# Row maxima of an attention kernel: split as columns, turned by the DVE, and started eight units earlier

## What is computed

```python
Q, K, V = (proj(Wq), proj(Wk), proj(Wv))          # x is (8, 512, 1024); 16 heads of 32
att = jnp.einsum('bhqd,bhkd->bhqk', Q, K) * (1.0 / math.sqrt(Dh)) + b[0]
att = att * m + (1.0 - m) * NEG_INF               # m: mask over the keys
att = jax.nn.softmax(att, axis=-1)
y = jnp.einsum('bhqk,bhkd->bhqd', att, V)         # then y back to (B, C, T)
q, in_scale = per_token_quant_int8(y)             # FFN: absmax per row, int8
out = (q @ weight.T) * in_scale * w_scale + bias  # cast to float16
return x + out
```

## Time and profile before

| | |
|---|---|
| median of 3 runs | 2440.25 us (2439.67 to 2441.79) |
| the profiled execution | 2440.84 us, of it 2439.0 us span from the first to the last instruction |
| TensorE busy | 2387.2 us, 98% of the span, at a mean granted clock of 0.993 |
| POOL, DVE, ScalarE busy | 1672.1, 1560.4 and 1346.3 us (69%, 64% and 55%) |
| chain of work that ended last | TensorE 67% of the span, DMA 4%, POOL and DVE 2% each |

### The profile page before, as it was taken

One profiled execution on the slowest core, in us unless ns is written; L12 is line 12 of the kernel. 1 busy time (PEld: TensorE's weight loads), 2 busy tenths in 40 slices (PEclk: granted clock), 3 DMA queues, 4 the chain that ended last, 5 costly groups with the idle time before them and its releaser, 6 DMA issues.

```text
span 2439.0 us, 37390 instructions
## 1 busy us (share of the span) xinstructions
PE 2387.2 (98%) x12376; PEld 1341.0 (55%) x12376; DVE 1560.4 (64%) x1683; ACT 1346.3 (55%) x2536; POOL 1672.1 (69%) x677
## 2 busy tenths in 40 slices
PE   8999999997999999999999999999999999999996
PEld 7888888884444444444444444444444444444442
DVE  3311111145777777777777777777777877777771
ACT  3222222214666666666666666666666666666664
POOL 3322223414778888888877888888788888887777
PEclk9999999998999999999999999999999999999999
DMA  6655555365677776777677777666776667776751
GB/s 243 252 200 199 214 193 195 147 211 126 147 160 160 157 157 147 157 159 159 151 159 159 156 160 156 157 151 150 160 160 155 155 150 160 160 155 154 157 111 44
DMA packets 143498, 396.55 MB, mean 163 GB/s; under 512 B 14584, under 2 KB 50424, under 8 KB 127296
## 3 DMA queue, kind: packets, MB, share of 16 engines
q0 software_dynamic: 18144, 132.13, 27.4%
q10 hardware_dynamic: 49312, 130.80, 22.8%
q1 hardware_dynamic: 75968, 132.74, 14.9%
HBM read 161.51 MB, written 100.93 MB: 108 GB/s over the span
## 4 chain that ended last, share of the span: by engine, by line
PE 67%; DMA 4%; issue 2%; POOL 2%; DVE 2%; ACT 0%; SPq 0%; ACTq 0%; POOLq 0%; DVEq 0%
PE score L689 21%; PE pv L716 18%; PE ring L127 18%; PE ring L749 4%; DMA q_stack<-max_lo 4%; PE ring L726 2%; PE ring L729 2%; DVE neg_max L136 1%; PE ring L740 1%; POOL acc L988 1%; PE ring L734 0%; DMA probs<-probs 0%; POOL acc L1000 0%; ACT probs L798 0%; SPq L609 0%
## 5 line engine op out<-in xcount | busy, mean ns | idle before, releaser
L798 ACT ACTIVATE probs<-score 128x512 f32<-128x512 f32 x2048 | 1074.7, 604 | 576.4 <-PE score L689 559.5
L136 DVE TENSOR_REDUCE neg_max<-ring 128x1 f32<-128x1024 f32 x1024 | 1208.4, 1220 | 230.8 <-PE ring L127 219.1
L689 PE MATMUL score<-q_stack,k_stack 100*128 100x512 f32 x2048 | 875.8, 429 | 23.9 <-DMA q_stack<-max_lo 16.6
L988 POOL TENSOR_TENSOR acc<-acc,probs 128x2048 f32<-128x2048 f32 x189 | 867.1, 4588 | 26.6 <-DMA probs<-probs 11.9
L127 PE MATMUL ring<-k_stack,q_stack 98*128 98x512 f32 x2048 | 810.6, 396 | 0.3 <-DVE neg_max L136 0.2
L689 PEld LDWEIGHTS score<-q_stack,k_stack 100*128 100x128 f32 x2048 | 387.3, 189 | 504.0 <-ACT probs L798 358.2
L716 PE MATMUL pv<-probs,v_in 128*32 128x512 f32 x4096 | 546.1, 605 | 0.0
L127 PEld LDWEIGHTS ring<-k_stack,q_stack 98*128 98x128 f32 x2048 | 390.8, 191 | 66.6 <-DVE neg_max L136 0.8
L988 POOL TENSOR_TENSOR acc<-probs 128x2048 f32<-128x2048 f32 x63 | 288.8, 4584 | 100.8 <-DMA probs<-probs 100.8
L479 POOL TENSOR_TENSOR q_stack<-x_raw,k_stack 128x1024 fp32r<-128x1024 f32 x28 | 67.7, 2450 | 294.7 <-ACT k_stack L364 294.7
L972 POOL DMA_DIRECT2D probs<-probs x126 | 108.2, 859 | 175.4 <-PE pv L716 168.2
(11 more groups left out here) (95 smaller groups left out, 2026.6 us busy)
## 6 DMA issues: line engine op xcount, KB each, us to landing
probs<-probs POOLq DMA_DIRECT2D x126, 1024.0 KB, 8.0
k_stack<-qk_part ACTq DMA_DIRECT2D x93, 512.0 KB
q_stack<-qk_part ACTq DMA_DIRECT2D x183, 256.0 KB, 5.4
qk_part<-part_hi SPq DMA_DIRECT2D x64, 512.0 KB, 2.6
qk_part<-part_lo SPq DMA_DIRECT2D x64, 512.0 KB, 3.5
v_steps<-v_out SPq DMA_DIRECT2D x64, 256.0 KB, 2.2
res<-x ACTq DMA_DIRECT2D x32, 512.0 KB, 5.7
out<-res SPq DMA_DIRECT2D x64, 256.0 KB, 2.1
```

The costliest lines, as they stand in the source:

```text
L136: nc.vector.tensor_reduce(neg_max[:, pair // CHUNK, pair % CHUNK:pair % CHUNK + 1], ring[:, :], AX_X, ALU.max, negate=True).then_inc(neg_m ...
L689: pe.matmul(score[score_bank(t)][:, :], k_stack[par][0:ROWS, h, kt * P:(kt + 1) * P], q_stack[par][0:ROWS, half, h, :], start=True, stop=T ...
L798: nc.scalar.activation(probs[:, kt, h, :], score[score_bank(t)][:, :], ACT.Exp).then_inc(exp_done, 1)
L988: nc.gpsimd.tensor_tensor(acc[:, half, :, :], first, probs[:, tile, :, :], ALU.add).then_inc(acc_done, 1)
```

## The change

OWN becomes 12, so each pair is made eight units earlier: 52 units of the step before hold pairs of a step, where 44 did. Chunk 1 is complete after unit 11 of its own step, chunk 0 after unit 43 of the step before. TensorE no longer turns the maxima. ScalarE and the DVE split the columns of `neg_max` where they stand (128 partitions by 16 columns), the DVE turns the two parts together, in blocks of 32 by 32, and SP writes them with four DMAs for each chunk, one for each 32 partitions. Before attention begins, 26 pairs are made where 22 were.

```diff
-OWN = 20
+OWN = 12
 EARLY = (UNITS - OWN) // 2
+MAXIMA_1, MAXIMA_0 = OWN - 1, OWN + UNITS // 2 - 1
...
+                    for pair in range(TT * 3 * CT // 4, EARLY):
+                        pe.wait_ge(neg_max_done, pair - 1)
+                        for half in range(2):
+                            row_max(pe, ring[pair % 2], q_stack, k_stack, 0, pair, half, rowmax_done)
...
-                for part, rows in ((0, max_hi), (1, max_lo)):
-                    dst = q_stack[par][ROW_MAX + part:ROW_MAX + part + 1, chunk, :, :]
-                    sp.dma_start(dst.bitcast(F32), rows[:, chunk, :].bitcast(F32)).then_inc(max_rows[chunk], 16)
+                rows = q_stack[par][ROW_MAX:ROW_MAX + 2, chunk, :, :].rearrange("r h (a g j) -> r h a g j", g=P // DH, j=DH)
+                for g in range(P // DH):
+                    sp.dma_start(rows[:, :, :, g, :].bitcast(F32), max_turned[g * DH:(g + 1) * DH, chunk, :]).then_inc(max_rows[chunk], 16)
...
-            def turn_max(s, chunk, buf):
-                pe.wait_ge(neg_max_done, PAIRS * s + CHUNK * (chunk + 1))
-                pe.transpose(buf[0:CHUNK, N:N + P], neg_max[:, chunk, :], ident[:, :]).then_inc(maxT_done, 1)
-
...
-            def high_max(s, chunk, buf):
-                act.wait_ge(maxT_done, 2 * s + chunk + 1)
-                wait(act, max_rows[chunk], MAX_ROWS * s)
-                nc.scalar.activation(max_hi[:, chunk, :], buf[0:CHUNK, N:N + P], ACT.Copy).then_inc(max_hi_done, 1)
+            def high_max(s, chunk):
+                act.wait_ge(neg_max_done, PAIRS * s + CHUNK * (chunk + 1))
+                wait(act, max_turn_done, 2 * (s - 1) + chunk + 1)
+                nc.scalar.activation(max_parts[:, chunk, 0, :], neg_max[:, chunk, :], ACT.Copy).then_inc(max_hi_done, 1)
...
-                    if t == SUMS_1 and main:
-                        high_max(s, 1, ring_of(par, ("extra", SUMS_1)))
+                    if t == MAXIMA_1 + 3 and main:
+                        high_max(s, 1)
...
+            def turn_max(s, chunk):
+
+                dve.wait_ge(max_lo_done, 2 * s + chunk + 1)
+                wait(dve, max_rows[chunk], MAX_ROWS * s)
+                nc.vector.transpose(max_turned[:, chunk, :],
+                                    max_parts[:, chunk, :, :].rearrange("p a b -> p (a b)").bitcast(F32)).then_inc(max_turn_done, 1)
...
-                    if t == SUMS_1 and main:
-                        low_max(s, 1, ring_of(par, ("extra", SUMS_1)))
+                    if t == MAXIMA_1 + 2 and main:
+                        low_max(s, 1)
+                        turn_max(s, 1)
+                    if t == MAXIMA_0 + 2 and ahead:
+                        low_max(s + 1, 0)
+                        turn_max(s + 1, 0)
```

More of the change, by code:

```diff
@@ L659, in wait_ring @@
                 elif t in (SUMS_1, SUMS_0):
-                    wait(pe, sums_out, 2 * s + (t == SUMS_0))
-                    if not isinstance(s, int) or s + (t == SUMS_0) < STEPS:
-                        pe.wait_ge(max_lo_done, 2 * s + (2 if t == SUMS_1 else 3))
+                    pe.wait_ge(sums_out, 2 * s + (t == SUMS_0))
                 elif t == TURN_Q:
@@ L671, in take_ring @@
                     pe.wait_ge(neg_max_done, EARLY)
-                    wait(pe, max_lo_done, s + 1)
                 else:
@@ L861, in step @@
                         make_ints(s - 1, (t - 41) // 2)
-                    if t == SUMS_0 and ahead:
-                        high_max(s + 1, 0, ring_of(par, ("extra", SUMS_0)))
-            act.wait_ge(const_set, 5)
+                    if t == MAXIMA_0 + 3 and ahead:
+                        high_max(s + 1, 0)
+            act.wait_ge(const_set, 4)
             act.wait_ge(stack_set, 4)
@@ L946, in step @@
                             scale_product(s - 1, half, ring_of(par, ("extra", FFN)))
-                    if t == SUMS_0 and ahead:
-                        low_max(s + 1, 0, ring_of(par, ("extra", SUMS_0)))
                     if t == SUMS_0 and main:
```

52 lines of the change are left out of this document (20 added, 32 removed).

## The result

The changed kernel takes 2562.88 us (median of 4 runs, 2553.88 to 2563.49), beside 2440.54 us for the kernel before on the same chip (4 runs, 2439.67 to 2441.79): a ratio of 1.0492, 95% interval 1.0469 to 1.0516. It is slower, as forecast, but by 122 us in place of 39, outside the range.

A forecast was written before the change was run, and what follows sets the result against it. TensorE's own instructions, in their order, were taken to set the time. Turns -21.7, old waits -9.8, K wait +56, DVE +12, ScalarE, SP and start +2 gave +38.5 on 2440.25: 2479 us, range 2460 to 2506.

The forecast's parts named there:

- The turns, the old waits, the start: Turns leave TensorE, -21.7 us; old waits for rows of maxima go, -9.8; ScalarE, SP and the start, +2.
- K at unit 12: TensorE at unit 12 waits for the next step's K and bias, 1.8 us in 31 steps: +56 us (+14 to +82).
- loads in time: Rival, chance 0.06: K and bias land by 1444.8, so no wait at unit 12; 2423 us.
- The DVE in unit 45: Subtraction and turn between reductions of units 45 and 47 delay unit 48: +12 us (0 to 22).
- unit 13 costs nothing: The same DVE pair at unit 13 has a unit more of slack: nothing (6 us if it had none).
- The clock: Rival, 0.16: K stalls also cost clock, 1.7 us each; 2505 us if in half of 31 steps, 2532 in all.
- The stores: Rival, 0.05: turned rows' stores land late, scores 32 wait about 1 us in 31 steps; 2510 us.

The follow-up runs named there:

- The run with unit 12 alone: Kernel before the change with row maxima started at unit 12 in place of 20, split and turn left on TensorE: 2512.18 us, ratio 1.0284.
- the run of the reciprocal: Changed kernel with the subtractions in slots 13 and 45 replaced by a reciprocal of the same shape, low part of the maxima left out: 2502.93 us, ratio 1.0251.
- the turn in unit 51: Changed kernel with the DVE's subtraction and turn of chunk 0 moved from unit 45 to unit 51: 2485.48 us, ratio 1.0176.
- the one with cut transfers: Changed kernel with row maxima from unit 16 and POOL's 1 MB transfers cut to 32 KB, the rest of those sums left out: 2403.73 us, ratio 0.9844.

## Why the prediction was right and wrong

**The turns, the old waits, the start.** Right: 2.71 for 3.06 us at the sums, no wait at scores 32, first score 2.6 us later (forecast 2).

**K at unit 12.** Right: +56 forecast, 44.0 us of waiting and some 49 us of lost time measured, 31 times. The landing that it worked out, 1446.4, is 11.1 us into its step; in the changed kernel the matmul that waits starts at 1496.41, 11.1 us into its step too. The run with unit 12 alone has it without the rest. The rival "loads in time" fell. The estimate of 1.8 us rested on K's volume and on the bias rows behind it; issuing those rows first took 0.7 us of the wait away and left 0.9, so both were in it.

**The DVE in unit 45.** This step failed: "I take 0.5 us for both", +12 (0 to 22), against 50 us. The two instructions themselves were sized rightly: the turn has 0.21 us, the subtraction 0.16 us where nothing holds it. That unit 13 costs nothing was right too (0.17 us there). What I left out is that moving an operation from PSUM to SBUF, and from slot 55 to slot 45, puts it under POOL's running addition, and that it stands until this addition ends. With an operation that POOL doesn't hold, the wait is 8.1 us, so the term was sound but for the hold. The trace of before could not show it: its subtraction had an input in PSUM and lasted 277 to 280 ns, under POOL's operations too. But POOL's additions could be read there, and the Trainium skill's rule (SBUF — State Buffer, Who interferes with whom), with which the run of the reciprocal agrees (0.25 us), would have made this a rival.

**The clock.** The sum put it at nothing, and kept it as a rival at 0.16. It came about, at up to 44 us, between the half and the whole of the rival's price. But that price was for the K stall alone; by itself that stall lost 25 us (the turn in unit 51), the half, and the rest came with the second stall, which the prediction had as 0.4 us a step only. I had weighed 2.24 us (lost) against 1.56 us (not lost) and counted on most stalls staying below 2.24. They did, at 1.4 to 1.5 us in the mean and 2.1 at most, and lost the clock all the same, in 25 stretches. The rule cited there from the Trainium skill (TensorE: Matmul & The Clock Gate, Why this matters for your kernels), by which no such gap would lower the clock, is not borne out: one of 1.45 us was followed by 0.50. One of 1.43 us was not, and what decides between them stays open.

**The stores.** A rival at 0.05, by landings of up to 8.2 us. The change itself was spared: its rows take 7.4 us, for POOL's second transfer comes late, and land 6.9 us ahead of score 32. For the later starts it decides: 71 us from unit 16, 105 from unit 20.

Sum by its steps: K 7 us too high, the DVE 38 us too low, the clock, 44 us, left out. That makes 75 us, as much as the profiled execution (2553.88 us) lies above the forecast; the median lies 84 above it.

## What to carry to other kernels

Before an operation of VectorE is moved, see what POOL is doing in the new slot, and whether the operation reads two tensors of SBUF or is a `tensor_scalar`: both, at 128x16, took here what was left of POOL's instruction. A start that is moved forward takes its loads' deadline with it, and small transfers take the time of the large ones of other queues that they share the way with: here the rows of chunk 1 took 3.9 us beside transfers of 32 KB, 7.2 to 8.2 us where one of 1 MB was issued within 1 us of them and the next over 2.5 us later or not at all, and 12 to 14 us between two, each within 2 us. A stall of TensorE hides others behind it: here taking one away (K's load, K's order, POOL's transfer) each time uncovered the next, and only a run that removes them all shows what a change is worth.

Whether the turn on VectorE can gain in a kernel that does all the work stays open. Only the run without K's third load and with the turn in unit 51 (2425.55 us) and the one with cut transfers (2403.73 us) are below the kernel before; the best whole ones took 2452 and 2455 us. With the start at 12 the rows land 6.9 us ahead of score 32 with the K stall and 6.2 us without K's third load and the stall, so there they are no hindrance; with the bias rows first that start took 2459 us. K's loads issued by SP ran with the start at 14 only.

## What was not expected of the hardware

- A VectorE subtraction of 128x16 in SBUF lasted 0.16 to 4.33 us over these runs, by what was left of POOL's instruction; a reciprocal and a transpose in the same slots 0.25 and 0.21 us.
- Four DMAs of 4 KB, issued 1.9 us behind a 1 MB transfer of another queue and 0.8 us ahead of a second, were there 13.5 us after their first issue; with the second transfer 3.9 us behind them, 7.4 us; with transfers of 32 KB, 3.9 us.
- Stalls of 1.4 to 1.8 us were followed by TensorE at half clock in many steps; in the run with stalls of 0.9 us a step the mean clock was 0.994, that of the kernel before 0.993.
